# Table lookups by halves of 256 samples between the work of the tiles, and the layers one tile behind

## What is computed

```python
e = jnp.stack([tbl_0[ids[:, 0]], ..., tbl_26[ids[:, 26]]], axis=1)     # 2048 x 27 x 128
dot = jnp.einsum('bnd,bmd->bnm', e, e)
z = dot.reshape(2048, 27 * 27)[:, idx]                                  # the 351 pairs i < j
h = jnp.concatenate([z, dense_ctx], axis=1)                             # 2048 x 367
h = jnp.maximum(h @ W_top1 + b_top1, 0.0)                               # 512 wide
h = jnp.maximum(h @ W_top2 + b_top2, 0.0)                               # 256 wide
y = h @ W_top3                                                          # 1 wide
```

## Time and profile before

| | us |
|---|---|
| median of 3 executions | 409.7 (406.43 to 410.01) |
| the profiled execution | 413.21 |
| its span in the profile | 411.4 |
| mean granted TensorE clock | 0.954 |

### The profile page before, as it was taken

How to read it: one execution, slowest core, us unless ns; L and a number is a source line. 1 busy time by engine, 2 the same in 40 slices (tenths; PEclk the granted TensorE clock), 3 DMA queues, 4 the chain that set the end, 5 groups by cost and what they waited for, 6 DMA issues and landing times.

```text
span 411.4 us, 9707 instructions
## 1 busy us (share of the span) xinstructions
PE 352.9 (86%) x3696; PEld 308.0 (75%) x3696; DVE 205.0 (50%) x420; ACT 118.6 (29%) x190; POOL 282.0 (69%) x280
## 2 busy tenths in 40 slices
PE   0698887685898999979889999979998999988838
PEld 0566666575786889979768889969876889978836
DVE  0799983111297982212469991212488982212100
ACT  1444423201222324223213324323221324232212
POOL 5778887777777777777777777777777777760000
PEclk9999999966999999969989999989998999999978
DMA  8999612654348422453556412454557312442120
GB/s 208 245 221 235 181 46 62 131 131 89 96 93 172 110 53 53 91 134 104 124 111 177 102 49 56 90 123 109 125 114 170 100 51 55 89 106 48 36 49 0
DMA packets 71566, 44.61 MB, mean 108 GB/s; under 512 B 53906, under 2 KB 60434, under 8 KB 71524
## 3 DMA queue, kind: packets, MB, share of 16 engines
q1 hardware_dynamic: 61038, 24.96, 27.7%
q0 software_dynamic: 8704, 17.84, 17.0%
q10 hardware_dynamic: 1782, 1.21, 1.1%
HBM read 38.11 MB, written 5.87 MB: 107 GB/s over the span
## 4 chain that ended last, share of the span: by engine, by line
PE 52%; POOL 19%; SPq 11%; issue 8%; DMA 6%; ACT 1%; ACTq 1%; DVE 1%; DVEq 0%; POOLq 0%
POOL rows L359 19%; PE ps_hot L513 12%; PE ps_hot L515 12%; PE ps_h L554 7%; PE ps_h L573 5%; PE ps_hot L541 5%; PE ps_dot L541 5%; PE ps_tr L525 4%; SPq L253 4%; SPq L255 4%; SPq L321 2%; DMA hot_ids<-in_hot_ids 2%; PE ps_h L588 2%; DMA zT<-dots_scratch 1%; DMA rows<-in_tbl,cold_ids 1%
## 5 line engine op out<-in xcount | busy, mean ns | idle before, releaser
L359 POOL DMA_INDIRECT rows<-in_tbl,cold_ids x272 | 281.1, 1034 | 85.5 <-issue 82.6
L513 PE MATMUL ps_hot<-onehot,table_hi 125*128 125x512 f32 x336 | 135.4, 403 | 25.6 <-DVE onehot L381 21.2
L381 DVE TENSOR_SCALAR onehot<-hot_ids,row_number 125x512 fp32r<-125x512 int32 x336 | 148.9, 489 | 11.6 <-PE ps_hot L515 6.7
L515 PE MATMUL ps_hot<-onehot,table_lo 125*128 125x512 f32 x336 | 133.9, 399 | 0.0
L513 PEld LDWEIGHTS ps_hot<-onehot,table_hi 125*128 125x128 f32 x336 | 65.0, 193 | 44.4 <-issue 20.9
L450 ACT COPY eT<-ps_hot 128x512 f32<-128x512 f32 x40 | 45.9, 1147 | 120.6 <-PE ps_hot L515 120.6
L515 PEld LDWEIGHTS ps_hot<-onehot,table_lo 125*128 125x128 f32 x336 | 64.9, 193 | 13.2
L393 DVE COPY eT<-ps_tr 128x512 f32<-128x512 f32 (+1 forms) x40 | 25.2, 630 | 85.8 <-PE ps_tr L525 85.8
L554 PE MATMUL ps_h<-zT,w 128*128 128x128 f32 x360 | 53.7, 292 | 9.0 <-DMA zT<-dots_scratch 5.7
L525 PE MATMUL ps_tr<-ident,rows 128*128 128x128 f32 x272 | 46.5, 294 | 12.3 <-DMA rows<-in_tbl,cold_ids 10.2
L554 PEld LDWEIGHTS ps_h<-zT,w 128*128 128x128 f32 x360 | 48.7, 207 | 10.0 <-DMA zT<-dots_scratch 6.2
(11 more groups left out here) (32 smaller groups left out, 79.6 us busy)
## 6 DMA issues: line engine op xcount, KB each, us to landing
hot_ids<-in_hot_ids SPq DMA_DIRECT2D x40, 256.0 KB
dots_scratch<-dots SPq DMA_DIRECT2D x62, 87.8 KB
rows<-in_tbl,cold_ids POOLq DMA_INDIRECT x272, 2.8
zT<-dots_scratch SPq DMA_DIRECT2D x48, 58.5 KB
dots<-in_tbl SPq DMA_DIRECT2D x3, 448.0 KB
dots<-in_tbl SPq DMA_DIRECT2D x2, 560.0 KB
dots_scratch<-dots SPq DMA_DIRECT2D x62, 1.6 KB
w<-in_tbl SPq DMA_DIRECT2D x2, 448.0 KB
```

Source lines behind the costliest of these rows:

```text
L359: pool.indirect_dma_start(out=rows[t][:, f, :], out_offset=None, in_=x["cold"][f][:, :], in_offset=bass.IndirectOffsetOnAxis(ap=cold_ids[: ...
L381: dve.tensor_scalar(onehot[:, c % NO, :], hot_ids[h % NI][0:CR, :], row, None, ALU.is_equal).then_inc(onehot_ready, 1)
L513: pe.matmul(ps_hot[h % 2][:, :], table_hi[:, c, :], onehot[:, c % NO, :], start=(c == FROM[h]), stop=False)
L515: pe.matmul(ps_hot[h % 2][:, :], table_lo[:, c, :], onehot[:, c % NO, :], start=False, stop=(c == FROM[h + 1] - 1)).then_inc(onehot_used, 1)
```

## The change

**Tables.** `HOT` gets an eleventh table (18, of 1250 rows): 94 chunks instead of 84. A tile has 16 gathers instead of 17, four groups of four. Transposes are in four groups of four, and `eT` has 38 columns a sample instead of 37.

**First lookups.** Samples 0 to 511 are looked up before all tiles, 512 wide as before (`first_lookups`). For each table chunks 5 and 7 are made on ScalarE, in two passes over 125 x 512 each: the distance |id - row|, then relu(1 - distance). VectorE makes the others. The ring holds five one-hots of this width. GpSimd waits before tile 3 until nine tables are split, since `rows[3]` is one of the places where tables are staged.

**Later lookups.** The other 1536 samples are looked up in six rounds of 256 samples, 94 chunks each and 256 columns wide, during tiles 2 to 13: 47 chunks to a tile, written between its steps by the table `DONE` (6 after each of the four groups of transposes, 4 after the products, 5 after layer 1, 6 after layer 2, 8 after layer 3). VectorE makes them all, up to five ahead of TensorE's place in the tile (`LEAD`), in a ring of ten. Tiles 0, 1, 14 and 15 have no lookups. Ids come in loads of 256 samples to eight slots, 66 of them.

**Products.** One matmul now takes one sample: 27 weight columns, 27 moving columns. Four samples lie beside each other at output rows 0, 32, 64 and 96. A tile has 128 matmuls, in two banks of their own; `ps_hot` is no longer used for them. VectorE and ScalarE copy one bank each. On tiles 0, 1, 4, 5, 8, 9, 12 and 13 the gathered and the looked-up columns lie in the other order, and the copy and the stores are in two pieces there (`pieces`): nine stores instead of five.

**Layers.** All three layers of tile k-1 are in tile k behind the products. Loops are written out (no hardware loop). Weights w1 and w2 are loaded behind the last table, as their buffers stage tables.

The diff, cut:

```diff
-HOT = [f for f in range(NF) if TABLE_ROWS[f] == 1000] + [26, 20]
+HOT = [f for f in range(NF) if TABLE_ROWS[f] == 1000] + [26, 20, 18]
...
+HALF = 2 * P
+NR = 4
+NI = 8
+NO = 10
...
+SHARE = NCH // 2
+DONE = [SHARE * s // 47 for s in (6, 12, 18, 24, 28, 33, 39, 47)]
+TR, PRODUCTS, LAYER1, LAYER2, LAYER3 = 0, 4, 5, 6, 7
+
+LEAD = 5
+
+SCALAR_CHUNKS = (5, 7)
...
+        def chunks_before(k, s):
+            if k < 2:
+                return NCH
+            return min(NCH * (k // 2) + SHARE * (k % 2) + (DONE[s - 1] if s else 0), NL)
...
+        def copy_products(copy, k, q):
+            for slot, count, row in pieces(k):
+                last = copy(dots[:, k % 2, slot:slot + count, HG * q:HG * q + HG],
+                            ps_dot[q][:, :, row:row + count].rearrange("p g i -> p i g"))
...
+                for slot, count, row in pieces(k):
+                    to = scratch[k % 2][1 + RP * slot:1 + RP * (slot + count), SG * s:SG * s + SG]
+                    at = SG * s + row
+                    engine.dma_start(to.rearrange("(j i) g -> j i g", i=RP), dots[at:at + count, k % 2, 1:NF, :])                      .then_inc(dots_stored[k % 2], 16)
...
+            for k in range(NT):
+                i = k % 2
+
+                free = [e for e in range(loaded, NH * (NU - 1)) if chunks_through(ids_before(e)) <= chunks_before(k, PRODUCTS)]
+                for e in free[0:len(free) // 2]:
+                    load_hot_ids(e)
+                if k >= 2:
+                    sp.wait_ge(z_ready[i], 16 * KC * uses(k))
+                sp.wait_ge(dot_read[0], k + 1)
+                sp.wait_ge(dot_read[1], k + 1)
+                store_dots(sp, k, range(2) if k == LAST else range(4))
...
+                sp.dma_start(zT[i][KP:P, 0, :], x["dense"][0:D0, samples]).then_inc(dense_ready[i], 16)
+                sp.dma_start(zT[i][KP:KP + D1, 1, :], x["dense"][D0:ND, samples]).then_inc(dense_ready[i], 16)
+                sp.wait_ge(dots_stored[i], stored(k + 2))
+                for c in range(KC):
+                    pairs = bass.AP(scratch[i].tensor, (JC * c * (RP + 1) + 1) * P,
+                                    [[(RP + 1) * P, JC], [P, NDIST], [1, P]])
+                    sp.dma_start(zT[i][0:KP, c, :], pairs).then_inc(z_ready[i], 16)
+                for e in free[len(free) // 2:]:
+                    load_hot_ids(e)
+                loaded += len(free)
+                if k:
+                    store_y(k - 1)
...
+            for k in range(NT):
+                if k in (0, NR):
+                    pool.wait_ge(cold_ids_ready[k // NR], 16)
+                if k == NR - 1:
+
+                    pool.wait_ge(lo_ready, max(range(0, NH, NB)) + 1)
+                for g in range(NG):
+                    if k >= NR:
+                        pool.wait_ge(transposed, NG * (k - NR) + g + 1)
+                    for f in group(g):
+                        pool.indirect_dma_start(
+                            out=rows[k % NR][:, f, :], out_offset=None, in_=x["cold"][f][:, :],
+                            in_offset=bass.IndirectOffsetOnAxis(ap=cold_ids[:, k, f:f + 1], axis=0),
+                        ).then_inc(rows_ready[k % NR][g], 16)
...
+            def first_onehots(h):
+                dve.wait_ge(first_ids_ready[h % (NI // 2)], 16 * (h // (NI // 2) + 1))
+                for c in chunks(h):
+                    if c - FROM[h] in SCALAR_CHUNKS:
+                        continue
+                    if c >= NO // 2:
+                        dve.wait_ge(onehot_used, c - NO // 2 + 1)
+                    row = row_number[0:CR, KINDS.index(CHUNKS[h]), c - FROM[h]:c - FROM[h] + 1]
+                    dve.tensor_scalar(first_onehot(c), first_ids(h)[0:CR], row, None, ALU.is_equal)\
+                       .then_inc(onehot_ready, 1)
+
...
+                    dve.wait_ge(onehot_used, max(n - NO + 1, NCH))
+                    row = row_number[0:CR, KINDS.index(CHUNKS[h]), c - FROM[h]:c - FROM[h] + 1]
+                    dve.tensor_scalar(onehot[:, n % NO, :], hot_ids[0:CR, ids_slot(e), :], row, None, ALU.is_equal)\
+                       .then_inc(onehot_ready, 1)
...
+            for h in range(NH):
+                split_low(h)
+                first_onehots(h)
+            made = NCH
+            for k in range(NT):
+                for g in (1, 3):
+                    upto = max(made, min(chunks_before(k, TR + g) + LEAD, NL))
+                    onehots(made, upto)
+                    made = upto
+                    transposed_out(k, g)
+                upto = max(made, min(chunks_before(k, LAYER1) + LEAD, NL))
+                onehots(made, upto)
+                made = upto
+                dve.wait_ge(dot_done[0], k + 1)
+                if k >= 2:
+                    dve.wait_ge(dots_stored[k % 2], stored(k))
+                copy_products(dve.tensor_copy, k, 0).then_inc(dot_read[0], 1)
...
+            def first_onehots(h):
+                act.wait_ge(first_ids_ready[h % (NI // 2)], 16 * (h // (NI // 2) + 1))
+                for k in SCALAR_CHUNKS:
+                    c = FROM[h] + k
+                    if c >= NO // 2:
+                        act.wait_ge(onehot_used, c - NO // 2 + 1)
+                    act.activation(first_onehot(c), first_ids(h)[0:CR], ACT.Abs,
+                                   bias=minus_row[0:CR, KINDS.index(CHUNKS[h]), k:k + 1]).then_inc(distance_ready, 1)
+                    act.wait_ge(distance_ready, scalar_made(c))
+                    act.activation(first_onehot(c), first_onehot(c), ACT.Relu, bias=one[0:CR, :], scale=-1.0)\
+                       .then_inc(scalar_onehot_ready, 1)
...
+            for k in range(NT):
+                transposed_out(k, 0)
+                lookups_out(k, 0)
+                lookups_out(k, 1)
+                transposed_out(k, 2)
+                lookups_out(k, 2)
+                lookups_out(k, 3)
+                act.wait_ge(dot_done[1], k + 1)
+                if k >= 2:
+                    act.wait_ge(dots_stored[k % 2], stored(k))
+                copy_products(act.copy, k, 1).then_inc(dot_read[1], 1)
+                if k == LAST:
...
+                lookups_out(k, PRODUCTS)
+                if k:
+                    hidden1(k - 1)
+                lookups_out(k, LAYER1)
+                if k:
+                    hidden2(k - 1)
+                lookups_out(k, LAYER2)
+                if k:
+                    output(k - 1)
+                lookups_out(k, LAYER3)
...
+            def lookups(start, stop):
+                for n in range(start, stop):
+                    c = n % NCH
+                    h = table_of(c)
+                    e = NH * (n // NCH) + h
+                    if c == FROM[h]:
+                        pe.wait_ge(hot_read, e - 1)
+                    pe.wait_ge(onehot_ready, n + 1 - scalar_made(n))
+                    pe.matmul(ps_hot[e % 2][:, 0:HALF], table_hi[:, c, :], onehot[:, n % NO, :],
+                              start=(c == FROM[h]), stop=False)
+                    pe.matmul(ps_hot[e % 2][:, 0:HALF], table_lo[:, c, :], onehot[:, n % NO, :],
+                              start=False, stop=(c == FROM[h + 1] - 1)).then_inc(onehot_used, 1)
+
+            def lookups_between(k, s):
+                lookups(chunks_before(k, s), chunks_before(k, s + 1))
...
-                for k in (2 * q, 2 * q + 1):
-                    if not (first and t == 0):
-                        pe.wait_ge(dot_read[k % 2], bank_reads(n, t, k) - 1)
-                    for g in range(BS):
-                        for c in range(2):
-                            s0 = 2 * (SG * c + BS * k + g)
-                            own = eT[:, t % 2, s0:s0 + 2, :].rearrange("d s a -> d (s a)")
-                            e = eT[:, t % 2, s0:s0 + 2, column0(t):column0(t) + NF]
-                            last = pe.matmul(banks[k][SC * c:SC * c + SC, WN * g:WN * g + WN],
-                                             own[:, column0(t):column0(t) + SC], e, start=True, stop=True)
-                    last.then_inc(dot_done, 1)
...
+                if k:
+                    pe.wait_ge(dot_read[q], k)
+                at = column0(k)
+                for g in range(HG):
+                    for s in range(4):
+                        e = eT[:, k % 2, SG * s + HG * q + g, at:at + NF]
+                        last = pe.matmul(ps_dot[q][SG * s:SG * s + NF, g, 0:NF], e, e, start=True, stop=True)
+                last.then_inc(dot_done[q], 1)
...
+            for h in range(NH):
+                first_lookups(h)
+            for k in range(NT):
+                for g in range(NG):
+                    transposes(k, g)
+                    lookups_between(k, TR + g)
+                products(k, 0)
+                products(k, 1)
+                lookups_between(k, PRODUCTS)
+                if k == 1:
+                    pe.wait_ge(w1_ready, 16 * (KC + 1))
+                    pe.wait_ge(w2_ready, 16)
+                    pe.wait_ge(w3_ready, 16)
```

(8 more changed lines are left out.)

542 lines of the change are left out of this document (223 added, 319 removed).

## The result

The changed kernel takes 483.6 us (median of 4, 481.2 to 489.7), the kernel before 409.9 us (median of 4, 406.4 to 410.8). The ratio is 1.180, with a 95% interval of 1.169 to 1.191: 18% slower. The forecast was 395 us, in a range that ended at 433. The profiled execution took 485.6 us, its span is 483.7.

A forecast was written before the change was run, and what follows sets the result against it. TensorE's own work, with holes, bounds the middle; tile 2 starts at 93, twelve tiles of 22.0 us reach 357, the last two 376, plus tail 20: span 396, 398 with the 1.8 around it, scaled to 395 us; range 375 to 433.

The forecast's parts named there:

- Products: 128 matmuls per tile at 0.027 us each: 3.4 us, 0.6 less than before; bounds 2.0 and 8.0 us.
- The half-clock row: Kernel before: the same 64 product entries take 3.67 us instead of 2.08, read as the array setting the pace.
- the rate of the queue: Two weight loads within 40 ns after a 0.32 us dry spell, read as matmuls can be fed under 40 ns each.
- Rival A: Products cost by the matmul: 8.0 us a tile, 469 us; decides from 4.3 us per tile; chance 0.22 with values between.
- The first stage: First lookups with the eleventh table end at 63 us instead of 60.3, ScalarE being waited for in seven tables; bounds 59, 67.
- Tile by tile: Twelve full tiles of 22.0 us: lookups 11.0, transposes and layers 6.9, products 3.4, small waits 0.7.
- Lookups of 256 columns: Later lookups on TensorE: 0.117 us per matmul, between 0.110 and 0.23; 1128 matmuls make 132 us, against 114 before.
- rival B: A 256-column lookup costs 0.15 us: 37 us more, 432 us; chance 0.07.
- Hidden work: zT's way of 15 us hidden within a tile; gathers out at 353 us, 17 us to spare before tile 15.
- rivals C and D: C: gathers late, at 1.45 us each, 410 us, chance 0.10. D: zT late in 14 tiles, 437 us, chance 0.11.
- The tail: Time behind the last products: 20 us, from 23.4 less about 3.5 as only one layer chain is left.
- The clock: TensorE's clock near 1.0 from 95 us to 370, as lookups fill what was idle and cold.

The follow-up runs named there:

- the versions with few entries: Changed kernel with one matmul of 54 moving columns per two samples (products partly wrong): 443.3 us; with paced loads and both start edits added: 411.9 us.
- the one of 412 us: Changed kernel with halved product matmuls (partly wrong), paced table-number loads, no ScalarE one-hots in the first stage, none ahead in the first tile: 411.9 us, ratio 1.007.

## Why the prediction was wrong

**The step that failed is the term "Products", 3.4 us a tile, with the rate 27 ns and the bound of 8.0 above it.** The price between holes was right, 54.8 us by 16 = 3.4 us a tile or 27 ns for a matmul of the program, though partly by luck: it is 18 ns and short pauses that nobody foresaw. What the term left out is that this very rate is faster than the program is brought. The blocks took 97.6 us by 16 = 6.1 us a tile, of which 2.7 were hole. The half-clock row said that the array sets the pace of 64 by 54 matmuls; it was taken to hold for 27 by 27 too, whose pace hardly changes with the clock (12.1 and 13.8 ns). I had read the rate of the queue from 40 ns behind the one place where it had run dry, two loads in that time, and taken it for what can be kept up over the 512 entries of a tile. It says how fast TensorE takes entries that are there. How fast they come no row of the kernel before showed, since its products use 256 entries in 4.0 us and so stay just under the supply of 256 in 3.1 to 3.8. (The stop of 0.32 us in the earlier trace rows stands at instruction 887, which is not 193 and a multiple of 256; it looks like the short pauses of the changed kernel, but its cause is open.) Rival A had the size (8.0 us a tile, 469 us) and its threshold was right: the products went over 4.3 us a tile, and the kernel was slower. Its mechanism was not: the price isn't paid by each matmul, as fewer entries a microsecond, or fewer altogether, make it vanish. The Trainium skill's 62 ns for each MATMUL (TensorE: Matmul & The Clock Gate, Wait — 56ns, not 53.3ns?), which the prediction set beside this rival, did not bind these products: 3.4 us a tile between holes, not 7.9.

**The late pieces** were in no rival. 12 to 21 us of the miss are the burst of six loads of table numbers that SyncE issues behind zT: 12 by pacing them, 21 by cutting them to an eighth. I had counted these loads as DMA that nothing on the path waits for; the path did, through TensorE's program.

**The first stage** was forecast to end at 63 us (59 to 67) and ended at 81.5, an error of 18.5. The term was ScalarE's pass of 512 at 0.55 us, made from a cast of 1024 in 1.05 us; it took 0.71 and 0.72. Four passes are 2.86 us, not 2.2. The remaining 1 us a table is the order: the second pass waits for the first by a semaphore, the table's copy and the next cast stand in one row with them, and TensorE's waits for ScalarE's one-hots (18.8 us for the weight loads of L568, above) cost clock as well, 0.87 in this stretch. How that 1 us divides was not tested. Without ScalarE's one-hots the stage ended at 67.3, so the change's own idea was worth less than nothing here: ScalarE's pair of passes takes 1.43 us for what VectorE does in 0.42.

**Tile by tile**, 22.0 us, was right for the kernel it described: 22.1 to 22.5 us in the versions with few entries. Lookups of 256 columns at 0.12 us (forecast 0.117, bounds to 0.23) were right; rival B is out. Small changes between lookups and other work, at up to 0.2 us, were not in the sum, and neither was VectorE's 0.30 us for a one-hot (171.3 by 564, forecast 0.26), for which TensorE's lookups idled 5.2 us in all.

**Hidden work** was as forecast. TensorE waited 2.2 us in all for zT and for no gathered rows (rivals C and D are out); the last gather was out at 383.5 us in the long kernel and at 342.0 in the one of 412 us, against a forecast of 353. The tail was 19.8 us, forecast 20.

**The clock** was forecast near 1.0 from 95 us on and was 0.94 in the steady part, with stretches at 1.2 GHz behind the long holes and behind one of 1.5 us. By the mean of the run, the time at the lower level is 0.184 x 483.7 = 89 us, against 38 in the kernel before.

The miss of 88 us, each part as the runs gave it: 15 first stage, 5 wait in the first tile, 12 to 21 late pieces, and the rest up to 72 the other holes, the longer blocks and the clock behind them. These parts overlap and were not measured as a sum. The 17 us between 395 and 412 are the first stage's later end (5 us), 0.5 us in each of 12 tiles (6 us), 3 us of the span elsewhere, and 3 us because the forecast was scaled down from the span and this run's median was not under its profiled execution. On the Trainium skill: Runtime: NRT & Kernel Launch, Instruction fetch mechanics, says that an engine's program is refilled in blocks of 16 KiB or 256 instructions, and calls the cost of crossing a block mostly hidden. The trace agrees with the first, by the spacing of the holes and 50 packets of 16 KB, and for this kernel not with the second: 42.8 us of 483.7.

## What to carry to other kernels

Count the instructions that an engine uses up in its densest stretch, not only their time: here a whole piece of 256 of them had to last 3.1 to 3.8 us. Stops came in the products used up at some 7 ns an entry, none at 15, and next to none at 12, where a tile's products are no more than one piece. Halving only one operand of a matmul saved little or nothing (31 to 30.2 and 24.7 ns), halving both more than half; and two narrow ones for one wide one can lose in the supply of instructions what they save in the array. Bursts of loads that nobody waits for delayed the program's own pieces: issue them a few at a time. And look where in the program the stops stand before giving them to the work that they interrupt.

## What the runs showed of the hardware

- TensorE's program came in packets of 16 KB, 256 instructions, 3.3 us apart at the closest; the holes stood exactly 256 instructions, or a multiple, apart (18 of 18 within products). A packet started 0.9 to 1.6 us after the piece before was entered, where nothing delayed it, and the next piece was used 2.2 to 2.8 us after that start.
- The packet waited for a burst of other DMA: it started up to 4.9 us after the piece before was entered (339.68 and 344.60), and the longest hole went from 5.6 to 3.0 us when two loads instead of six were under way.
- A matmul of the products, by the block: 13.4 ns at 27 stationary and 27 moving columns, 14.5 at 32 and 27, 24.7 at 27 and 54, 30.2 at 64 and 27, 31 at 64 and 54. At half clock the widest took 1.8 times as long (29.7 and 53.3), the narrowest 1.15 times (12.1 and 13.8). The first two shapes write to four places of the output rows in turn, the others to two.
- Going from lookups of 128 x 256 to products of 27 x 27 and back cost about 0.2 us beyond their own time, 0.19 by one timeline and 0.13 to 0.24 by the difference of two kernels.
- On one chip the kernel before took 699 us, and on the same chip some twelve minutes later 408.8; of the engines' work TensorE's was late. Why is open.
